# Two PSUM seeds on ScalarE in place of eight TensorE matmuls a block, a ring of sixteen scan units, and a new table of places

## The reference

```python
xn = _layernorm(x)
# branch 1: a Mamba block with 512 inner channels and 16 states
xz = rmsnorm(xn) @ in_proj_w.T;  x_s, z = split(xz)
u = silu(causal_conv(x_s, conv_w, 4 taps) + conv_b)
dt_raw, B, C = split(u @ x_proj_w.T)
delta = softplus(dt_raw @ dt_proj_w.T + dt_proj_b)
h_t = exp(delta * A) * h_{t-1} + (delta * u) * B     # for each channel and state
y = sum_s h * C + u * D_param
out1 = (y * silu(z)) @ out_proj_w.T + xn
# branch 2: a mixture of 8 experts, top 2 of each token
out2 = sum_e weight_e * (silu(xn @ w1_e.T) * (xn @ w3_e.T)) @ w2_e.T
return x + out1 + out2
```

## Time and profile before

| | |
|---|---|
| median of 3 runs | 2634.42 us (2634.39 to 2645.27) |
| profiled execution, its own time | 2637.98 us |
| its span | 2636.2 us |
| mean granted TensorE clock | 0.937 of full speed |
| DMA | 379.24 MB, mean 144 GB/s |

### The profile page before, as it was taken

The page is one execution under the profiler, slowest core; times in us unless marked ns, Lnnn a source line. Parts: engine busy times, 40 slices in busy tenths (PEclk is TensorE's granted clock), DMA queues, the critical chain, the costliest instruction groups (busy, mean ns, idle before and its releaser), DMA issues. The chain is left out here.

```text
span 2636.2 us, 44811 instructions
## 1 busy us (share of the span) xinstructions
PE 2292.0 (87%) x14442; PEld 1989.8 (75%) x14442; DVE 2350.0 (89%) x3113; ACT 1486.6 (56%) x3049; POOL 2035.6 (77%) x1607
## 2 busy tenths in 40 slices
PE   3968689999999999999999899999998999998665
PEld 2965478888887888878888878888887878886554
DVE  7679899999898999899999989989898998989886
ACT  3850555656656565656655565565556556565442
POOL 3340588888888888888888888888888888888763
PEclk7868789999999999999999999999999999999776
DMA  6315035555555556555555555555555555552541
GB/s 212 105 57 179 29 98 162 165 167 156 156 163 157 156 161 174 158 159 160 149 169 155 163 169 161 156 160 153 160 159 171 159 158 161 150 152 59 94 89 35
DMA packets 271178, 379.24 MB, mean 144 GB/s; under 512 B 21492, under 2 KB 166516, under 8 KB 270948
## 3 DMA queue, kind: packets, MB, share of 16 engines
q1 hardware_dynamic: 240292, 332.26, 40.1%
q0 software_dynamic: 28480, 43.94, 9.7%
q10 hardware_dynamic: 2176, 0.18, 0.1%
HBM read 332.59 MB, written 52.10 MB: 146 GB/s over the span
## 5 line engine op out<-in xcount | busy, mean ns | idle before, releaser
L1138 DVE TENSOR_TENSOR_SCAN h<-DA,carry,h 128x512 f32<-128x512 f32 x600 | 764.7, 1276 | 47.1 <-POOL h L550 24.3
L1364 PE MATMUL HT<-ident,h 128*128 128x128 f32 x2912 | 474.8, 292 | 182.0 <-DVE W L1155 93.9
L1364 PEld LDWEIGHTS HT<-ident,h 128*128 128x128 f32 x2912 | 358.6, 150 | 286.2 <-issue 259.2
L550 POOL TENSOR_TENSOR h<-W,bbc 128x512 f32<-128x512 f32 x300 | 408.9, 1400 | 91.9 <-PE HT L1364 42.9
L550 POOL TENSOR_TENSOR h<-du,bbc 128x512 f32<-128x512 f32 x300 | 408.0, 1414 | 88.2 <-PE HT L1364 50.1
L1138 DVE TENSOR_TENSOR_SCAN W<-DA,carry,W 128x512 f32<-128x512 f32 x296 | 377.3, 1276 | 26.0 <-POOL W L550 13.2
L1155 DVE SCALAR_TENSOR_TENSOR W<-HT,cT,W 128x512 f32<-128x512 f32 x480 | 349.5, 728 | 1.4 <-PE HT L1364 1.3
L1155 DVE SCALAR_TENSOR_TENSOR yT<-HT,cT,yT 128x512 f32<-128x512 f32 x480 | 349.3, 728 | 0.0
L817 ACT ACTIVATE DA<-delta,alog 128x512 f32<-128x512 f32 x448 | 302.2, 685 | 29.5 <-DVE h L1138 18.4
L817 ACT ACTIVATE DA<-W,alog 128x512 f32<-128x512 f32 x448 | 302.1, 685 | 28.6 <-DVE h L1138 19.0
L1423 PE MATMUL G<-W,fill 128*128 128x256 f32 x1080 | 274.3, 400 | 0.0
(11 more groups left out here) (227 smaller groups left out, 4307.2 us busy)
## 6 DMA issues: line engine op xcount, KB each, us to landing
W<-in_w_T_dram SPq DMA_DIRECT2D x405, 512.0 KB
bbc<-b_dram SPq DMA_DIRECT2D x256, 256.0 KB
xraw<-in_x_dram SPq DMA_DIRECT2D x64, 256.0 KB, 2.9
xn_dram<-W SPq DMA_DIRECT2D x8, 1032.0 KB, 14.5
W<-in_x_dram SPq DMA_DIRECT2D x32, 256.0 KB, 6.5
moe_dram<-fill SPq DMA_DIRECT2D x32, 256.0 KB, 3.9
out_dram<-tmpA SPq DMA_DIRECT2D x32, 256.0 KB, 2.1
out_dram<-moe_dram POOLq DMA_DIRECT2D x32, 256.0 KB, 4.4
```

The lines of the kernel that those rows point to most:

```text
L550: pool.tensor_tensor(h(g), du_pair[n // 2 % 2][:, k, :], bbc[:, g // 4 % BRING, :], ALU.mult).then_inc(s_dbu, 1)
L1138: i = dve.tensor_tensor_scan(h(g), DA[:, g % 2, :], h(g), carry[:, b, s, k:k + 1], ALU.mult, ALU.add)
L1364: i = pe.transpose(HT[:, g % 2, c * P:(c + 1) * P], src, ident[:, :])
```

## The change

- `copy_xs` no longer copies the bias to PSUM: for each channel group it computes last tap x xs + bias with one ScalarE activation of 256 columns (two where there was one copy of 512). `conv` runs three matmuls a channel group instead of four, and cwd has three taps.
- A new `seed_y` on ScalarE writes D/2 x (2u) to FA or FB, two activations of 256 columns for each half; the matmuls with dskip go. `y_mm` waits for s_sy (the seed) instead of s_z; the seed waits for s_z and s_u.
- GROUPS goes from 3 to 4 (`h_later`, in the place of `xrT_late` and `xr_late`, which get memory of their own), AHEAD from 4 to 8 for long units. `product_at` says in which of its steps GpSimd makes a product: four units before at the first unit of a pair, two products a step from there until it is eight ahead; short units stay at four.
- `normalise(3)` no longer waits for s_xnd (the store of the normalised rows); ScalarE's first `first_state` of the long stage does. LEAD (loads of B rows ahead) goes from 2 to 3, INDEX and GATHER one unit earlier.
- The table moves: MULT 4 to 5, SCATTER 8 to 9, XT_UNITS, and many places of FRONT and BACK. `due` and `tiles_at` become look-ups while the program is built.

```diff
-    AHEAD = 4
-    GROUPS = 3
+    AHEAD = 8
+    GROUPS = 4
...
-    LEAD = 2
+    LEAD = 3
...
-        cwd = sb("cwd", [P, CH, TAPS, P])
-        dskip = sb("dskip", [P, CH, P])
+        cwd = sb("cwd", [P, CH, TAPS - 1, P])
...
+        product_at = []
+        for g in range(UNITS):
+            first = U * first_of_block(g)
+            at = max(g - (AHEAD if is_long(g // U) else 4), first - 4 + (g - first) // 2 if is_long(g // U) else 0)
+            product_at.append(max(at, product_at[-1] if g else -1) if g > 3 else -1)
...
-        FRONT = {"normalise": 6, "transpose": 7, "copy_xT": 8, "xs0": 8, "copy_xs0": 9, "xs1": 10, "copy_xs1": 12,
-                 "conv0": 11, "conv1": 12, "conv2": 13, "conv3": 14, "tanh_u0": 13, "silu_u0": 14, "tanh_u1": 15, "silu_u1": 16,
-                 "x_proj": 17, "copy_xdbc": 18, "store_b": 19, "dt": 19, "abs": 20, "exp": 22, "ln": 23, "sp0": 24, "sp1": 25,
-                 "wm": 23, "corr": 24, "delta": 26, "du": 27, "cT": 25, "copy_cT": 26}
-        BACK = {"z0": -1, "tanh_z0": 0, "silu_z0": 1, "z1": 2, "tanh_z1": 3, "silu_z1": 4, "y0": 4, "gate_y0": 6, "y1": 5,
-                "gate_y1": 7, "reload": 7, "oacc": 26, "out0": 27, "out1": 28, "result": 30}
+        FRONT = {"normalise": 6, "transpose": 7, "copy_xT": 8, "xs0": 8, "copy_xs0": 11, "xs1": 9, "copy_xs1": 13,
+                 "conv0": 11, "conv1": 11, "conv2": 13, "conv3": 14, "tanh_u0": 14, "silu_u0": 15, "tanh_u1": 16,
+                 "silu_u1": 17, "x_proj": 17, "copy_xdbc": 18, "store_b": 18, "dt": 19, "abs": 21, "exp": 21, "ln": 23,
+                 "sp0": 24, "sp1": 25, "wm": 22, "corr": 23, "delta": 27, "du": 27, "cT": 24, "copy_cT": 26}
+        BACK = {"z0": -2, "tanh_z0": 0, "silu_z0": 1, "z1": 0, "tanh_z1": 2, "silu_z1": 3, "seed_y0": 2, "y0": 3,
+                "gate_y0": 5, "seed_y1": 3, "y1": 5, "gate_y1": 9, "reload": 7, "oacc": 27, "out0": 27, "out1": 28,
+                "result": 32}
...
-        XT_UNITS = (4, 13, 18, 23, 30)
+        XT_UNITS = (3, 13, 19, 23, 30)
...
-        INDEX, GATHER = -5, -4
-        XT, XT_COPY, H1, H3, TANH, A2, MULT, Y, YO, SCATTER = 0, 1, 2, 3, 3, 4, 4, 5, 6, 8
+        INDEX, GATHER = -6, -5
+        XT, XT_COPY, H1, H3, TANH, A2, MULT, Y, YO, SCATTER = 0, 1, 2, 3, 3, 4, 5, 5, 6, 9
...
-                if g + AHEAD < UNITS:
-                    make_dbu(g + AHEAD)
+                for u in range(g, min(g + AHEAD + 1, UNITS)):
+                    if product_at[u] == g:
+                        make_dbu(u)
...
-                if n == 3:
-                    act.wait_ge(s_xnd, 16 * (TILES // 8))
...
-                act.copy(src[:, :, :], cb[:, 2 * q:2 * q + 2].unsqueeze(2).to_broadcast([P, 2, T])).then_inc(s_seed, 1)
+                for m in range(2):
+                    c = 2 * q + m
+                    i = act.activation(src[:, m, :], xs[:, c, HALO:HALO + T], ACT.Identity, bias=cb[:, c:c + 1],
+                                       scale=cw[:, c, TAPS - 1:TAPS])
+                i.then_inc(s_seed, 1)
+
+            def seed_y(n, q):
+
+                act.wait_ge(s_z, 2 * n + q + 1)
+                act.wait_ge(s_u, 2 * n + 2)
+                if n == 0 and q == 0:
+                    act.wait_ge(s_prep, NPREP)
+                for m in range(2):
+                    c = 2 * q + m
+                    i = act.activation((FA if q else FB)[:, m, :], u2(n)[:, c, :], ACT.Identity, scale=hdpar[:, c:c + 1])
+                i.then_inc(s_sy, 1)
...
+                if n == LONG:
+                    act.wait_ge(s_xnd, 16 * (TILES // 8))
...
-                for k in range(TAPS):
-                    i = pe.matmul(dst, cwd[:, c, k, :], xs[:, c, k:k + T], start=False, stop=(k == TAPS - 1),
+                for k in range(TAPS - 1):
+                    i = pe.matmul(dst, cwd[:, c, k, :], xs[:, c, k:k + T], start=False, stop=(k == TAPS - 2),
                                   skip_group_check=True)
...
-                pe.wait_ge(s_z, 2 * n + q + 1)
+                pe.wait_ge(s_sy, 2 * n + q + 1)
                 dst = FA if q else FB
-                for m in range(2):
-                    c = 2 * q + m
-                    pe.matmul(dst[:, m, :], dskip[:, c, :], u2(n)[:, c, :], start=(m == 0), stop=False,
-                              skip_group_check=True)
```

More of the change, by code:

```diff
@@ L94, in build @@
         spot += 4 * 2 * T
+        h_later = late[:, spot:spot + 4 * 2 * T].rearrange("p (r t) -> p r t", r=4)
+        spot += 4 * 2 * T
         yT_late = late[:, spot:spot + 2 * NT * DI].rearrange("p (k d) -> p k d", k=2 * NT)
         spot += 2 * NT * DI
-        xrT_late = late[:, spot:spot + KD * T].rearrange("p (k t) -> p k t", k=KD)
-        spot += KD * T
-        xr_late = late[:, spot:spot + NT * DM].rearrange("p (t d) -> p t d", t=NT)
         scratch = [W[:, part + i * 1024:part + (i + 1) * 1024] for i in range(8)]
@@ L176, in build @@
          s_route, s_tot, s_cnt, s_slot, s_oh, s_xtr, s_xtT, s_h1, s_h3, s_th, s_a2, s_ha,
-         s_y2, s_yo, s_sc, s_mz, s_add, s_gate, s_iota, s_inv, s_gt, s_ix, s_idx, s_nw, s_bias, s_seed, s_y0) = [sem(n) for n in """
+         s_y2, s_yo, s_sc, s_mz, s_add, s_gate, s_iota, s_inv, s_gt, s_ix, s_idx, s_nw, s_bias, s_seed, s_y0, s_sy) = [sem(n) for n in """
             s_par s_prep s_id s_x s_xres s_xn s_oacc s_tr s_xT s_xsmm s_zmm s_xs s_halo s_conv s_tu
@@ L226, in xrT @@
         def xrT(n):
-            return xrT_own[:, n % 4] if n % 4 < 3 else xrT_late
+            return xrT_own[:, n % 4]
         def xr(n):
@@ L310, in tiles_at @@
         def tiles_at(g, stage):
[L312 to L315, removed]
+            return TILE_AT.get(g - stage)
         def fills(i, ring):
             return i // ring + 1
-        FRONT = {"normalise": 6, "transpose": 7, "copy_xT": 8, "xs0": 8, "copy_xs0": 9, "xs1": 10, "copy_xs1": 12,
-                 "conv0": 11, "conv1": 12, "conv2": 13, "conv3": 14, "tanh_u0": 13, "silu_u0": 14, "tanh_u1": 15, "silu_u1": 16,
-                 "x_proj": 17, "copy_xdbc": 18, "store_b": 19, "dt": 19, "abs": 20, "exp": 22, "ln": 23, "sp0": 24, "sp1": 25,
-                 "wm": 23, "corr": 24, "delta": 26, "du": 27, "cT": 25, "copy_cT": 26}
-        BACK = {"z0": -1, "tanh_z0": 0, "silu_z0": 1, "z1": 2, "tanh_z1": 3, "silu_z1": 4, "y0": 4, "gate_y0": 6, "y1": 5,
-                "gate_y1": 7, "reload": 7, "oacc": 26, "out0": 27, "out1": 28, "result": 30}
+        FRONT = {"normalise": 6, "transpose": 7, "copy_xT": 8, "xs0": 8, "copy_xs0": 11, "xs1": 9, "copy_xs1": 13,
[5 more added lines that the diff above has]
+                "result": 32}
         AT = {(name, n): U * max(n - 2, 0) + at for name, at in FRONT.items() for n in range(1, NB)}
@@ L339, in build @@
[L339 to L343, removed]
+        END = U * (NB - LONG)
@@ L344, in build @@
+        place_at(NB - 1, z0=END + 44, tanh_z0=END + 45, silu_z0=END + 46, z1=END + 47, tanh_z1=END + 48, silu_z1=END + 49, seed_y0=END + 48, seed_y1=END + 51, reload=END + 41)
         LOAD_X = {2: 7, 3: 32, 4: 40}
         LOAD_X.update({n: AT["oacc", n - 5] + 1 for n in range(5, NB)})
-        ADD_AT = {n: 946 + 2 * n for n in range(NB - 4)}
-        ADD_AT.update({NB - 4: 1002, NB - 3: 1004, NB - 2: 1010})
-        XT_UNITS = (4, 13, 18, 23, 30)
+        ADD_AT = {n: END - 14 + 2 * n for n in range(NB - 4)}
@@ L350, in build @@
+        ADD_AT.update({NB - 4: END + 42, NB - 3: END + 44, NB - 2: END + 50})
+        DUE = {}
+        for (name, n), at in sorted(AT.items()):
+            DUE.setdefault((name, at), []).append(n)
+        XT_UNITS = (3, 13, 19, 23, 30)
         LOGITS, ROUTE = U + 2, U + 3
-        INDEX, GATHER = -5, -4
-        XT, XT_COPY, H1, H3, TANH, A2, MULT, Y, YO, SCATTER = 0, 1, 2, 3, 3, 4, 4, 5, 6, 8
+        INDEX, GATHER = -6, -5
+        XT, XT_COPY, H1, H3, TANH, A2, MULT, Y, YO, SCATTER = 0, 1, 2, 3, 3, 4, 5, 5, 6, 9
@@ L354, in build @@
         W1_LOAD, W3_LOAD, W2_LOAD = 4, 5, 7
         def due(name, g):
-            return [n for n in range(NB) if AT.get((name, n)) == g]
+            return DUE.get((name, g), [])
+        TILE_AT = {tile_start(i): i for i in range(NTILES)}
         block = ctx.enter_context(nc.Block())
@@ L603, in _ @@
             make_du(0)
-            for g in range(AHEAD):
+            for g in range(4):
                 make_dbu(g)
@@ L892, in step @@
                         tanh_z(n, q)
+                    for n in due(f"seed_y{q}", g):
+                        seed_y(n, q)
                 for n in due("oacc", g):
@@ L1182, in _ @@
             dve.wait_ge(s_par, NPAR)
[L1183 to L1186, removed]
+            for c in range(CH):
+                i = dve.tensor_tensor(cwd[:, c, :, :], ident[:, :].unsqueeze(1).to_broadcast([P, TAPS - 1, P]),
+                                      cw[:, c, 0:TAPS - 1].unsqueeze(2).to_broadcast([P, TAPS - 1, P]), ALU.mult)
+            i.then_inc(s_prep, 1)
             for at, to, by in ((0, R, 0.5), (R, R + NS, 0.25), (R + NS, ROWS, 0.5)):
```

22 lines of the change are left out of this document (13 added, 9 removed).

## The result

The changed kernel takes **2467.49 us** in the median, 0.9353 of the time before (95% interval 0.9324 to 0.9381). The median counts one execution of 7989.63 us, which the ratio leaves out; the other three took 2466.32 to 2468.65 us. The profiled execution took 2466.34 us, its span is 2464.6.

What follows compares the result with a forecast made beforehand. VectorE's in-order queue was taken as the bound, with 174.9 us of idle time to win; long-stage terms of -87 and -5 at the end gave -92, so 2542 us against 2634.42, range 2490 to 2612.

Steps and rivals of the forecast that it cites:

- TensorE's relief: Long stage: 111 us less TensorE work, worth nothing by itself, showing up in waits as earlier H1, H3 and convolution.
- slower rivals: ScalarE's queue holding dA up in units 2 and 3, 2686 us at 65% exposed, 5%; lower granted clock, 2790 us, 3%.
- B: TensorE in lock-step with VectorE over HT; half the gain returns as waits for dA, H1, gates; about 2590 us, 13%.
- H3's wait (MULT): Long stage: MULT one unit later clears VectorE's 109 waits for H3; -44 us, bounds 47.2 to 0 gained.
- tanh's wait (A2): Long stage: TensorE reaches H1 earlier, so waits for ScalarE's tanh of a tile halve; -18 us, bounds 0 to 37.6.
- products: Long stage: a stock of eight units covers GpSimd's late products, 27 waits; -34 us, bounds 0 to 37.5.
- smaller waits: Long stage: of VectorE's 17.2 us of smaller waits, silu of u and z among them, -6 us; bounds 0 and 17.
- dA: Long stage: VectorE's 35.4 us of waits for ScalarE's dA stay unchanged; bounds down to 15, up to 70.
- what surfaces: Long stage: some removed waits come back as others, TensorE staying as tight as before; +15 us, bounds 0 to 50.
- end: Passage from long to short units: first short units find groups freed four units earlier; -5 us.
- GpSimd's waits for turns: GpSimd's 93.1 us of waits in one of its groups remain, draining a stock of up to 18.9 us, not 9.4.
- ScalarE's 94 us: Seeds of the convolution and y add 2.94 us a block on ScalarE, 94 us over 32, beside VectorE's work.

Runs made afterwards that it cites:

- experiment 5: Changed kernel with ScalarE relieved: only the bias copied to PSUM, last tap and D u left out, TensorE as light as now; 2466.86 us.
- MULT alone: Kernel before with MULT one unit later (5 instead of 4) and nothing else; 2621.13 us, 0.9939.
- seeds alone, old places: Kernel before with both seeds on ScalarE, places of before for all but the last blocks, ring of twelve, products four ahead; 2591.66 us.
- seeds and ring, old places: Changed kernel with the places of before (MULT, GATHER, SCATTER, LEAD too) for all but the last blocks; 2568.73 us.
- table alone: Kernel before with the new places, stages and load edges, but four taps and D u on TensorE, ring of twelve, products four ahead; 2599.90 us.
- MULT taken back: Changed kernel with MULT one unit earlier, 4 instead of 5; 2564.35 us.
- TensorE's load put back: Changed kernel with TensorE's removed load issued again (tap 2 twice, two extra matmuls before the turns of y), ScalarE as changed; 2533.47 us.
- four ahead: Changed kernel with products four units ahead instead of eight, ring of sixteen kept; 2542.47 us.
- experiment 7: Changed kernel, moves added in turn: second softplus sum a unit earlier, 2465.53 us; normalisation at unit 5, 2464.25; second gate at unit 7, 2464.90.

## Why the prediction was wrong

**Bound and direction: right.** VectorE's queue set the time, its waits were the gain, TensorE's relief was worth something through them, ScalarE's 70 us cost nothing (experiment 5), and the clock stayed (0.99 in the long stage). None of the slower rivals came; B, with waits given back, didn't either.

**The sum, term by term.** Forecast -92, measured -171.6 on the span:

| term | forecast | measured |
|---|---|---|
| H3's wait (MULT) | -44 | -47.2 |
| tanh's wait (A2) | -18 | -30.5 |
| products | -34 | -37.5 |
| smaller waits | -6 | -10.3 |
| dA | 0 | -5.9 |
| what surfaces | +15 | none beyond the rows above |
| VectorE's own busy time | 0 | -27.4 |
| end | -5 | -12.0 |
| start | 0 | -0.8 |

**The step that failed first** is the sentence "Its own work isn't changed; all that the change can win in the long stage is a part of 174.9 us", and with it a term for VectorE's busy time, which the sum doesn't have. The stage lost 158.8 us, less than that ceiling, but only 131.4 of them are idle time; 27.4 came from VectorE's busy time. Back to back, a VectorE instruction begins before the one before it has ended. Three neighbours in the changed kernel:

```profile
1023.27 1.27 DVE L1167 TENSOR_TENSOR_SCAN W<-DA,carry,W 128x512 f32<-128x512 f32 x1
1024.46 0.73 DVE L1184 SCALAR_TENSOR_TENSOR W<-HT,cT,W 128x512 f32<-128x512 f32 x1
1025.10 0.68 DVE L1145 TENSOR_TENSOR fill<-fill,G 128x512 f32<-128x512 f32 x1
```

The scan of 1.27 us is followed after 1.19 us, the add of 0.73 after 0.64. Busy time counts what overlaps once. Each stop loses the overlap. Added up from the trace, VectorE's instructions last 2560.6 us before and 2556.8 after, nearly the same; they overlap by 210.6 us before and by 235.2 after. So 24.6 of the 28.4 us are overlap. Over the whole span, from the page and the sum of VectorE's waits:

| kernel | VectorE busy us | waits, us | waits, times |
|---|---|---|---|
| before | 2350.0 | 264.2 | 408 |
| MULT alone | 2342.9 | 249.5 | 344 |
| seeds alone, old places | 2342.3 | 229.3 | 334 |
| seeds and ring, old places | 2342.1 | 205.4 | 340 |
| table alone | 2336.0 | 236.8 | 232 |
| MULT taken back | 2331.6 | 211.8 | 246 |
| TensorE's load put back | 2329.2 | 176.4 | 180 |
| four ahead | 2327.1 | 186.7 | 180 |
| all three moves of experiment 7 | 2329.1 | 105.8 | 122 |
| changed kernel | 2321.6 | 119.7 | 120 |

288 stops fewer and 24.6 us more overlap: 0.085 us a stop, and a straight line through all fifteen kernels gives 0.087. The busy time follows the number of stops better than their length: the seeds and the ring at the old places wait less than the table alone and are busy for longer, with more stops. It isn't exact. The last run of experiment 7 has the changed kernel's number of stops and is busy for 7.5 us more; it has more breaks of under 0.15 us, which the waits don't count (185 for 160), and the rest is open. The prediction priced waits at their idle time, which is too little by a sixth when they are 0.5 us long.

**The second is "what surfaces", +15.** I took waits as things that come back elsewhere. Taken one at a time they do: MULT alone frees 47 us of waits and gives back 33 over the span (264.2 to 249.5 in all), and the ring at the old places is worth 23. The change moves all of them at once, and then little was left to step in. Not nothing: of the 29.5 us left for dA, 12.2 stand at unit 8 of the pairs, where the kernel before waited for H3 and tanh and not for dA. The sum has them in the row for dA, whose other waits fell by more. So the forecasts for H3 and the products (-44, -34) are near the rows, but neither is what the step earns by itself. Giving back half or more, as rival B would have it, is what MULT alone did.

**The third is the tanh, mis-sized** at half of its bound. Counted by unit, in us:

| kernel | tanh's waits | units 7, 8 | 17, 49 | 22, 54 | 27, 59 |
|---|---|---|---|---|---|
| before | 37.6 | 13.1 | 9.2 | 13.7 | 0 |
| seeds alone, old places | 13.7 | 0 | 0 | 13.7 | 0 |
| table alone | 39.9 | 3.5 | 32.4 | 0 | 3.8 |
| changed kernel | 7.1 | 4.3 | 0 | 0 | 2.8 |
| TensorE's load put back | 37.8 | 3.7 | 32.4 | 0 | 1.8 |

The seeds, and so TensorE's relief, take 23.9 us at the old places. The last 13.7, at units 22 and 54, stay with the seeds alone and go with the new places, and the new places alone put 32 us at units 17 and 49. The prediction let only the relief count, and at 0.8 us a tile at most, from an even share. That was the wrong measure: the load of the convolution lies just ahead of H1 at units 17 and 49, and put back it makes the 27 waits there 1.2 us long each.

**Two smaller readings.** GpSimd's waits for turns were to remain; over both tiles of the product they fell from 139.4 to 42.4 us in the long stage. And ScalarE's 94 us were added up from durations: its instructions do last 89 us longer in all, but they too overlap, and its busy time rose by 70.

The end's -12.0 was -5 in the forecast: besides the products' 9.3 us, waits for dA there fell from 4.6 to 1.8. Some of it is chance: the end took 172.1 and 165.1 us in the first two runs of experiment 7, which change nothing there. With the seeds alone it took 174.0.

## What to carry to other kernels

When several engines take turns at being late to one queue, changing one of them can earn a fraction of its waits, and changing all can earn more than the sum; a part judged alone on an already tuned table is judged too low (17 us for MULT alone, 97 for taking it out of the finished kernel, whose places are built on it). Count stops as well as their time: here each cost about 0.09 us beyond the idle time shown. And if the last waits move when they are filled with other work, the engine that releases them is the one to look at.

## What the hardware showed that was not expected

VectorE's overlap of 0.08 us between neighbouring instructions (1.27 us scans at a spacing of 1.19 us, adds of 0.73 at 0.64) is lost at each stop, so that "busy" of an engine whose work is unchanged moved by 1.2% between two kernels (2350.0 to 2321.6 us).
